# A Mamba2 layer between two mixtures of LoRA experts: x projected two steps further ahead and transposed on VectorE and by DMA

## The chip, the cores and the metric

One core of a Trainium2 chip runs the whole program. The metric is the device time of one execution in microseconds, the median of three runs. Everything is float32; the large products are made of three passes over rounded high parts and remainders (float32r).

## The reference

```python
x = x + 0.5 * ffn(layernorm(x))        # base_W, 8 LoRA experts of rank 16, top 2
x = x + attn(layernorm(x))
x = x + 0.5 * ffn(layernorm(x))
# attn, for x of [4, 256, 512]:
proj = x @ in_proj_w.T                  # gate 8192, xBC 8192+2*8*128, dt 128
xBC = silu(depthwise_conv4(xBC)); x, B, C = split(xBC)
dA = softplus(dt + dt_bias) * A; cs = cumsum(dA)        # chunks of 128 tokens
Y = (C.B * exp(cs_l - cs_s) * tril) @ (x * dt) + carried state + x * D
out = rms_norm(Y * silu(gate), per group of 1024) * norm_w @ out_proj_w.T
```

There are 128 heads of 64 channels in 8 groups; a group shares its B and C.

## The kernel before

Three phases run one after the other: a feed-forward block, the mixer, and a feed-forward block. The mixer takes some 1,430 of the 1,625 us and goes through 8 groups. A group has 16 steps (`STEPS`): a step is one channel tile of 128 channels (two heads, j = st//2) and one half of the tokens (512 tokens, two batches, hf = st%2). Every engine has its own order of work, written out by hand in `steps` and `tail`, and the engines meet at semaphores only.

The projections into the convolution are counted in units, 20 for a group (`UNITS`): 4 for B and C, and then one for each step's x. In a step st, unit st+5 is projected (`ip.project`, L842), taken out of PSUM by ScalarE (`ip.evacuate`, L865), given its three other taps by VectorE (`tap`, L882), passed through a tanh on ScalarE (`tanh_conv`, L1094) and made into silu on VectorE (`silu_conv`, L1240). The result stays in `acc`, which has 4 places.

TensorE's order in a step is: `transpose_x` (L1441: four transposes of 128x128 of x into the bank T_BANK), `ip.project` (12 matmuls), `project_gate` (L1451, 12 matmuls), `project_out` (L1482, 12 matmuls, from step 8 of the first group on) and `mix_tokens` (L1461, 16 matmuls; it raises the semaphore y). Between two groups, in `tail`, it projects units 1 to 5 of the next group, makes the products of B and C (`b_dot_c`, L1426) and sums squares over channels (`sum_over_channels`, L1501).

VectorE's order in a step is: `skip_y` (L1274) of the step before, which waits for y; `make_mix` (L1254); `scale_x` (L1264), x times dt out of T_BANK; the three taps; `silu_gate` (L1283); `silu_conv`; in odd steps `split_wo` (L1288); and in the steps 1 to 8 `add_quads` (L1305) and `add_group` (L1312). GpSimd's order in a step is: `mask_diagonals` (L1016), whose first half (L1021) waits for the rows of cs and its second half (L1025) for y; `gate_y` (L1030) of the step before; `remainder_w` (L837); `split_tile` (L1035); `sum_squares` (L1041). ScalarE: `decay_from_first` (L1100), `round_w` (L831), `evacuate`, `square` (L1133), `round_tile` (L1127), `decay_from_second` (L1111), `tanh_gate` (L1122), `tanh_conv`. SyncE issues all DMAs in one order: in a step the weights of the projection (`load_w`, L816), the rows of cs two steps ahead (`load_cs`, L973), and in odd steps `load_wo`.

Semaphores start at one, so 1 + STEPS * g + n reads "n steps of group g are done". `step_slot_freed` waits for the step before last, as most tiles have two places.

Of the kernel before, what the change touches and what calls it, by code (L numbers as in the profile page):

```python
# [605 lines left out]
class DtPart:  # L606
# [22 lines left out]
    def sync(self, sp):  # L629
# [161 lines left out]
class InProj:  # L791
# [3 lines left out]
    def __init__(self, nc, ctx, m, w_in, conv_w, conv_b, d_skip):  # L795
        def sb(name, shape, dt=F32):
# [4 lines left out]
            "const_in", "nw_in", "const", "proj", "gate", "xt", "y", "cb", "out", "ss",  # L801
# [14 lines left out]
    def load_w(self, sp, g, w):  # L816
        if not (first(g) and w < 3):
            sp.wait_ge(self.s["wlo"], 1 + WPG * g + w - 2)
        sp.dma_start(self.w_raw[:, w % 3, :, :], self.w_in[g, w, :, :, :]).then_inc(self.raw_in[w % 3], 16)
# [11 lines left out]
    def round_w(self, act, g, w):  # L831
        act.wait_ge(self.raw_in[w % 3], 16 * (WPG // 3 * g + w // 3 + 1))
        w_freed(act, self.s, g, w)
        self.nc.scalar.activation(self.w_hi[:, w % 3, :, :], self.w_raw[:, w % 3, :, :],  # L834
                                  ACT.Copy).then_inc(self.s["whi"], 1)
# [19 lines left out]
    def conv_constants(self, dve, g):  # L855
# [7 lines left out]
        dve.wait_ge(s["const"], 1 + 5 * g + 2)  # L863

    def evacuate(self, act, g, u):  # L865
# [34 lines left out]
def mixer_phase(nc, m, ip, norm_w, w_out, ncs_dram, next_ln):  # L900

    with ExitStack() as ctx:
# [4 lines left out]
        wo_in = [ctx.enter_context(nc.semaphore(f"mx_wo_in{i}")) for i in range(2)]  # L907
        cs_in = [ctx.enter_context(nc.semaphore(f"mx_cs_in{i}")) for i in range(2)]
# [17 lines left out]
        sq = sb("sq", [P, 2, HALF])  # L926
# [3 lines left out]
        B_UNIT, C_UNIT = 0, 1  # L930
# [677 lines left out]
```

## Time and profile before

| | |
|---|---|
| median of 3 runs | 1625.21 us (1624.32 to 1627.58) |
| profiled execution, its own time | 1627.01 us |
| span of the profiled execution | 1625.2 us, mean granted TensorE clock 0.989 |
| busy share of the span | TensorE 96%, VectorE 76%, GpSimd 65%, ScalarE 62% |
| transposes of x on TensorE (L1447) | 512, 84.3 us busy |
| DMA | 131.65 MB, 16 queues 24.3% busy |

The span runs from the first to the last instruction; the execution's own time is 1.8 us longer. Busy time of an engine is the union of its instructions; matmuls overlap each other, so that the sum of their durations is more than TensorE's busy time, and the distance from one start to the next is what a matmul costs. An instruction's duration holds what it waits inside, for a port for example, but not its wait for a semaphore, which the profile shows as idle time before it.

### The profile page before, as it was taken

To read this page: it belongs to the slowest core of one execution; us is meant where nothing else is said; L and a number is where in the kernel's file an instruction comes from. 1 tells how busy PE (TensorE), PEld (TensorE's weight loads), DVE (VectorE), ACT (ScalarE), POOL (GpSimd) and SP (SyncE) were. 2 spreads that over 40 slices of the span, in tenths; PEclk is the share of its full clock that TensorE was granted. 3 is DMA by queue.
4 is the path that set the end of the run, shared out by engine and by line. 5 is a ranking of instruction groups with operands and counts; after the bars stand their busy time and mean duration, and the time that the engine had idled before them with its cause. 6 is when DMAs were issued, how large, how long until landed. Compare 5 with 4: busy or idle time off the path is not lost. (4 is left out here: it accounts for less than half of the span.)

```text
span 1625.2 us, 25474 instructions
## 1 busy us (share of the span) xinstructions
PE 1564.3 (96%) x8296; PEld 1226.0 (75%) x8296; DVE 1228.0 (76%) x1689; ACT 1002.3 (62%) x2122; POOL 1052.0 (65%) x790
## 2 busy tenths in 40 slices
PE   6979999999999999999999999999999999999979
PEld 4657777777777777777777777777777777777757
DVE  6688877787778877887688877887688877887565
ACT  4357765666666665666666665666666665666431
POOL 2017874788757874788657874787657874787620
PEclk9899999999999999999999999999999999999989
DMA  3033321323222221222212321223222221322011
GB/s 118 1 103 103 107 91 59 92 91 92 78 72 92 92 92 59 91 92 92 78 72 92 92 91 59 92 92 92 78 75 88 92 92 59 98 86 84 20 40 53
DMA packets 73658, 131.65 MB, mean 81 GB/s; under 512 B 10944, under 2 KB 10944, under 8 KB 73280
## 3 DMA queue, kind: packets, MB, share of 16 engines
q1 hardware_dynamic: 73536, 130.09, 24.3%
q8 instruction: 68, 1.11, 0.3%
q14 instruction: 54, 0.44, 0.1%
HBM read 127.44 MB, written 2.62 MB: 80 GB/s over the span
## 5 line engine op out<-in xcount | busy, mean ns | idle before, releaser
L892 DVE SCALAR_TENSOR_TENSOR mx_acc<-bank,mx_cw,mx_acc 128x510 f32<-128x510 f32 (+2 forms) x480 | 358.3, 746 | 160.8 <-ACT mx_acc L877 149.5
L159 PE MATMUL bank<-h_hi,mx_w_hi 128*128 128x512 f32 x1152 | 465.6, 404 | 4.4 <-DVE mx_acc L892 2.3
L161 PE MATMUL bank<-h_hi,mx_w_lo 128*128 128x512 f32 x1152 | 453.1, 393 | 0.0
L160 PE MATMUL bank<-h_lo,mx_w_hi 128*128 128x512 f32 x1152 | 450.2, 391 | 0.0
L1108 ACT ACTIVATE mx_mix<-mx_csb,mx_gncs 128x256 f32<-128x256 f32 x512 | 218.9, 499 | 284.3 <-PE bank L1478 281.3
L1033 POOL TENSOR_TENSOR mx_y<-mx_y,mx_sg 128x512 f32<-128x512 f32 x128 | 338.4, 2644 | 59.7 <-DVE mx_y L1280 51.7
L839 POOL TENSOR_TENSOR mx_w_lo<-mx_w_raw,mx_w_hi 128x512 fp32r<-128x512 f32 x144 | 187.4, 1302 | 111.0 <-ACT mx_w_hi L834 111.0
L161 PEld LDWEIGHTS bank<-h_hi,mx_w_lo 128*128 128x128 f32 x1152 | 216.9, 188 | 48.5
L159 PEld LDWEIGHTS bank<-h_hi,mx_w_hi 128*128 128x128 f32 x1152 | 217.3, 189 | 47.8 <-issue 6.5
L160 PEld LDWEIGHTS bank<-h_lo,mx_w_hi 128*128 128x128 f32 x1152 | 217.7, 189 | 41.5
L1262 DVE TENSOR_TENSOR mx_mix<-mx_mix,mx_cbt 128x1536 f32<-128x1536 f32 x128 | 224.5, 1754 | 0.0
L1025 POOL TENSOR_SCALAR_AFFINE_SELECT mx_mix<-mx_csb 128x512 f32<-128x512 f32 x128 | 89.9, 702 | 202.0 <-PE bank L1478 202.0
L877 ACT ACTIVATE mx_acc<-bank,mx_cb,mx_cw 128x512 f32<-128x512 f32 x160 | 124.2, 777 | 140.9 <-PE bank L161 140.9
L159 PE MATMUL bank<-mx_wo_hi,mx_yt_hi 128*128 128x512 f32 x512 | 203.4, 397 | 7.3 <-POOL mx_yt_lo L1038 7.3
L1038 POOL TENSOR_TENSOR mx_yt_lo<-mx_y,mx_yt_hi 128x512 fp32r<-128x512 f32 x128 | 167.3, 1307 | 58.2 <-ACT mx_yt_hi L1131 58.0
L161 PE MATMUL bank<-mx_wo_hi,mx_yt_lo 128*128 128x512 f32 x512 | 202.0, 394 | 0.0
L160 PE MATMUL bank<-mx_wo_lo,mx_yt_hi 128*128 128x512 f32 x512 | 200.5, 392 | 0.0
L1021 POOL TENSOR_SCALAR_AFFINE_SELECT mx_csb<-mx_csb 128x512 f32<-128x512 f32 x128 | 123.2, 963 | 68.1 <-DMA mx_csb<-cs_rows 68.1
L1280 DVE SCALAR_TENSOR_TENSOR mx_y<-mx_acc,mx_dh,bank 128x512 f32<-128x512 f32 x128 | 95.3, 745 | 88.9 <-PE bank L1478 88.8
L1118 ACT ACTIVATE mx_mix<-mx_mix,mx_gncs 128x128 f32<-128x128 f32 x512 | 162.1, 389 | 0.0
L1474 PE MATMUL bank<-mx_mix,mx_xd 128*64 128x256 f32 x1024 | 160.5, 392 | 0.0
L1046 POOL TENSOR_TENSOR mx_ssum<-mx_ssum,mx_sq 128x512 f32<-128x512 f32 x112 | 148.2, 1323 | 1.1 <-ACT mx_sq L1140 1.1
(163 smaller groups left out, 2203.7 us busy)
## 6 DMA issues: line engine op xcount, KB each, us to landing
mx_csb<-cs_rows SPq DMA_DIRECT2D x128, 512.0 KB, 4.0
mx_w_raw<-in_w_in SPq DMA_DIRECT2D x144, 256.0 KB, 4.0
mx_wo_raw<-in_w_out SPq DMA_DIRECT2D x64, 256.0 KB, 4.2
res<-in_x SPq DMA_DIRECT2D x8, 256.0 KB, 5.0
f_base_raw<-in_base_wt SPq DMA_DIRECT2D x2, 1024.0 KB, 6.1
out<-res SPq DMA_DIRECT2D x8, 256.0 KB, 2.0
f_a_raw<-in_lora_a SPq DMA_DIRECT2D x2, 256.0 KB, 3.8
f_lb_raw<-in_lora_b SPq DMA_DIRECT2D x2, 256.0 KB, 6.2
```

Of the source, the lines that this page charges most:

```text
L159: nc.tensor.matmul(out, w_hi, x_hi, start=first, stop=False)
L160: nc.tensor.matmul(out, w_hi, x_lo, start=False, stop=False)
L161: return nc.tensor.matmul(out, w_lo, x_hi, start=False, stop=last)
L839: self.nc.gpsimd.tensor_tensor(self.w_lo[:, w % 3, :, :], self.w_raw[:, w % 3, :, :], self.w_hi[:, w % 3, :, :].bitcast(F32), ALU.subtract ...
L892: self.nc.vector.scalar_tensor_tensor(dst, src[:, :, 0:SEQ - k], self.cw[:, c, TAPS - 1 - k:TAPS - k], dst, ALU.mult, ALU.add).then_inc(s[ ...
L1033: nc.gpsimd.tensor_tensor(y[:, st, :], y[:, st, :], sg[:, st % 2, :], ALU.mult).then_inc(s["yg"], 1)
L1038: nc.gpsimd.tensor_tensor(yt_lo[:, p % 2, :, :], y_tile(q, hf, t), yt_hi[:, p % 2, :, :].bitcast(F32), ALU.subtract).then_inc(s["ylo"], 1)
L1046: nc.gpsimd.tensor_tensor(ssum[:, i, :], ssum[:, i, :], sq[:, i, :], ALU.add).then_inc(s["ssum"], 1)
L1108: nc.scalar.activation(mix[:, i, hd, b, 0:SEQ], csb[:, i, hd, b * SEQ:(b + 1) * SEQ], ACT.Exp, bias=gncs[:, tile, head:head + 1], scale=-1.0)
L1118: last = nc.scalar.activation(mix[:, i, hd, b, SEQ:PAIR], mix[:, i, hd, b, SEQ:PAIR], ACT.Exp, bias=gncs[:, tile, head:head + 1], scale=-1.0)
L1262: nc.vector.tensor_tensor(a, a, both, ALU.mult).then_inc(s["mix"], 1)
L1474: nc.tensor.matmul(Y_BANK[i][rows, c0:c0 + SEQ], xd[:, i, 2 * b, hd, :], mix[:, i, hd, b, 0:SEQ], start=True, stop=False)
```

## The change

Three things are changed together.

1. The lead of the projections goes from 5 to 7 units (`LEAD`, `ahead`): step st projects, evacuates and convolves unit st+7, so that units 0, 1 and 2 of the next group are made in the steps 13 to 15, and units 3 to 6 in the tail. Ahead of the first step of the first group stand units 3 to 6 too. The weights are loaded, rounded and split in a new order (`weight_order`), B's two halves before C's two.
2. TensorE transposes x no longer. VectorE transposes the squares of 32x32 of a unit into `th` (`turn_squares`), SyncE writes that tile to memory (`move_out`) and reads it back in four DMAs, one for each row of squares, into the new tile `xt` (`move_in`). `scale_x` reads `xt` in SBUF, where it read T_BANK.
3. The copies of the products of B and C (`keep_bc`) go from VectorE to ScalarE. The tile `sq` is gone: the squares go into `sg`, and `square` stands after `tanh_conv`. The decays read their constants from `m.ncs`, without the copy `gncs`. The loop of SyncE over the groups is written out.

```diff
+LEAD = 7
+def ahead(g, st):
+    u = st + LEAD
+    return (g, u) if u < UNITS else (g + 1, u - UNITS)
...
+def first_needed(g, st):
+    if st % 2 == 1:
+        return (g, 3 + st + 1) if st < STEPS - 1 else (g + 1, 2)
+    j = st // 2 + 2
+    return (g, 2 + 2 * j) if j < XT else (g + 1, (j - XT))
+def weight_order():
+    order = [(0, 0), (0, 1), (0, 2), (0, 4), (0, 3)]
+    for g in range(NG):
+        order += [first_needed(g, st) for st in range(STEPS)] + [(g + 1, 4), (g + 1, 3)]
+    return [(g, k) for g, k in order if g < NG]
...
+        xt = sb("xt", [P, 2, P // SQ, 2 * HB, SQ])
-        sq = sb("sq", [P, 2, HALF])
...
+            def move_out(g, st):
+                i, u = st % 2, st + 4
+                sp.wait_ge(s["turned"], 1 + STEPS * g + st + 1)
+                if not (first(g) and st < 2):
+                    x_moved(sp, *((g, st - 2) if st >= 2 else (g - 1, st + STEPS - 2)))
+                sp.dma_start(x_dram[i, :, :], th[:, u % 2, :]).then_inc(x_out[i], 16)
+            def move_in(g, st):
+                i = st % 2
+                step_slot_freed(sp, s["xd"], g, st)
+                sp.wait_ge(x_out[i], 16 * (XT * g + st // 2 + 1))
+                for q in range(P // SQ):
+                    src = x_dram[i, :, q * P:(q + 1) * P].rearrange("(i r) e -> r i e", r=SQ)
+                    sp.dma_start(xt[q * SQ:(q + 1) * SQ, i, :, :, :].rearrange("r i t c -> r i (t c)"),
+                                 src).then_inc(x_in[i], 16)
...
             def group(g, more):
                 for st in range(STEPS):
+                    ip.load_w(sp, 5 + WPG * g + st + 1)
                     if st + 2 < STEPS:
                         load_cs(g, st + 2)
...
+                    if 3 <= st + 2 < STEPS:
+                        move_in(g, st + 2)
+                    if st + 3 < STEPS:
+                        move_out(g, st + 3)
                 if more:
                     load_late(g + 1)
+                    ip.load_w(sp, 5 + WPG * g + STEPS + 1)
+                    ip.load_w(sp, 5 + WPG * g + STEPS + 2)
+                    for st in range(3):
+                        move_out(g + 1, st)
+                        move_in(g + 1, st)
```

On ScalarE, in `tanh_conv`:

```diff
+                if u >= 6:
+                    act.wait_ge(x_out[u % 2], 16 * (XT * g + (u - 6) // 2 + 1))
```

In a step of ScalarE:

```diff
                     tanh_gate(g, st)
+                    if gu < NG:
+                        tanh_conv(gu, un)
                     if st >= 1:
                         square(g, st - 1)
```

In the tail of ScalarE:

```diff
+                    evacuate(g + 1, 3)
+                    ip.round_w(act, 5 + WPG * g + STEPS)
                     square(g, STEPS - 1)
                     tanh_conv(g + 1, 3)
+                    keep_bc(g + 1, 0)
                     evacuate(g + 1, 4)
+                    ip.round_w(act, 5 + WPG * g + STEPS + 1)
                     tanh_conv(g + 1, 4)
+                    keep_bc(g + 1, 1)
+                    evacuate(g + 1, 5)
+                    tanh_conv(g + 1, 5)
                     root(g)
+                    evacuate(g + 1, 6)
+                    tanh_conv(g + 1, 6)
...
+            def turn_squares(g, st):
+                u = st + 4
+                dve.wait_ge(s["conv"], 1 + UNITS * g + u + 1)
+                nc.vector.transpose(th[:, u % 2, :].rearrange("p (q t c) -> p t q c", t=2 * HB, c=SQ),
+                                    acc[:, u % 4, :, :].rearrange("p b t -> p (b t)")).then_inc(s["turned"], 1)
             def scale_x(g, st):
-                dve.wait_ge(s["xt"], 1 + STEPS * g + st + 1)
+                x_moved(dve, g, st)
                 dve.wait_ge(s["y"], 1 + STEPS * g + max(st - 1, 0))
                 nc.vector.tensor_tensor(
-                    xd[:, i, :, :, :], T_BANK[:, :].rearrange("p (t h c) -> p t h c", h=2, c=HD),
-                    gdt[:, 4 * hf:4 * hf + 4, 2 * j:2 * j + 2].unsqueeze(3).to_broadcast([P, 4, 2, HD]),
-                    ALU.mult).then_inc(s["xd"], 1)
+                    xd[:, i, :, :, :].rearrange("p t h (i c) -> p (h i) t c", c=SQ), xt[:, i, :, :, :],
+                    gdt[:, hf, 2 * j:2 * j + 2, :, :].rearrange("p h i t -> p (h i) t").unsqueeze(3)
+                    .to_broadcast([P, P // SQ, 2 * HB, SQ]), ALU.mult).then_inc(s["xd"], 1)
```

In a step of VectorE, behind `silu_conv` and `split_wo` and ahead of `add_quads`:

```diff
+                    if gu < NG and un >= 4:
+                        turn_squares(gu, un - 4)
```

In the tail of VectorE:

```diff
                     taps(g + 1, 3)
                     silu_conv(g + 1, 3)
                     taps(g + 1, 4)
                     silu_conv(g + 1, 4)
+                    turn_squares(g + 1, 0)
+                    taps(g + 1, 5)
+                    silu_conv(g + 1, 5)
+                    turn_squares(g + 1, 1)
+                    mean_square(g)
+                    taps(g + 1, 6)
+                    silu_conv(g + 1, 6)
+                    turn_squares(g + 1, 2)
```

In a step of TensorE:

```diff
-                    transpose_x(g, st)
-                    if 0 < st < STEPS - 1:
-                        ip.project(pe, g, st + 5)
+                    if gu < NG:
+                        ip.project(pe, gu, un)
                     project_gate(g, st)
```

In the tail of TensorE:

```diff
                     ip.project(pe, g + 1, 3)
                     b_dot_c(g + 1, 0)
+                    ip.project(pe, g + 1, 4)
+                    sum_over_channels(g, 0)
+                    b_dot_c(g + 1, 1)
+                    ip.project(pe, g + 1, 5)
                     sum_over_channels(g, 1)
+                    ip.project(pe, g + 1, 6)
```

## Rows read from the trace of the kernel before

**Rows 1.** The page, busy time of each engine.

```profile
PE 1564.3 (96%) x8296; PEld 1226.0 (75%) x8296; DVE 1228.0 (76%) x1689; ACT 1002.3 (62%) x2122; POOL 1052.0 (65%) x790
```

**Rows 2.** Timeline of TensorE: start us, us, line, idle before; a step, and a tail's beginning.

```profile
705.36 0.66 PE L1447 MATMUL bank<-ident,mx_acc 128*128 128x128 f32 x4
...
706.09 0.40 PE L160 MATMUL bank<-h_lo,mx_w_hi 128*128 128x512 f32 x1
...
715.64 0.66 PE L1447 MATMUL bank<-ident,mx_acc 128*128 128x128 f32 x4
...
808.22 0.50 PE L159 MATMUL bank<-h_hi,mx_w_hi 128*128 128x512 f32 x1
808.56 0.39 PE L160 MATMUL bank<-h_lo,mx_w_hi 128*128 128x512 f32 x1
```

**Rows 3.** Timeline of TensorE: first transposes of four steps, two of the first group.

```profile
130.09 0.66 PE L1447 MATMUL bank<-ident,mx_acc 128*128 128x128 f32 x4 [0.56 <-DVE mx_acc L1244]
...
138.25 0.66 PE L1447 MATMUL bank<-ident,mx_acc 128*128 128x128 f32 x4 [0.56 <-DVE mx_acc L1244]
...
828.39 0.66 PE L1447 MATMUL bank<-ident,mx_acc 128*128 128x128 f32 x4 [1.71 <-DVE mx_acc L1244]
...
836.14 0.66 PE L1447 MATMUL bank<-ident,mx_acc 128*128 128x128 f32 x4
```

**Rows 4.** Timeline of VectorE and GpSimd in a step; then gate_y by line, min/median/max ns.

```profile
706.62 1.75 DVE L1262 TENSOR_TENSOR mx_mix<-mx_mix,mx_cbt 128x1536 f32<-128x1536 f32 x1
706.79 2.74 POOL L1033 TENSOR_TENSOR mx_y<-mx_y,mx_sg 128x512 f32<-128x512 f32 x1 [0.25 <-DVE mx_y L1280]
...
708.29 0.69 DVE L1269 TENSOR_TENSOR mx_xd<-bank,mx_gdt 128x512 f32<-128x512 f32 x1
...
L1033 POOL TENSOR_TENSOR mx_y<-mx_y,mx_sg x128: 1261/2734/2792, 122.6 to 1535.2; 128x512 f32<-128x512 f32 x128
```

**Rows 5.** Timeline of GpSimd and VectorE later in a step; then split_wo by line.

```profile
701.69 1.30 POOL L1046 TENSOR_TENSOR mx_ssum<-mx_ssum,mx_sq 128x512 f32<-128x512 f32 x1
...
702.65 0.89 DVE L1244 SCALAR_TENSOR_TENSOR mx_acc<-mx_th,mx_acc 128x512 f32<-128x512 f32 x1
...
702.94 1.09 POOL L1021 TENSOR_SCALAR_AFFINE_SELECT mx_csb<-mx_csb 128x512 f32<-128x512 f32 x1
...
703.46 1.11 DVE L1290 SCALAR_TENSOR_TENSOR mx_wo_lo<-mx_wo_raw,mx_nw,mx_wo_hi 128x512 fp32r<-128x512 f32 x1
...
L1290 DVE SCALAR_TENSOR_TENSOR mx_wo_lo<-mx_wo_raw,mx_nw,mx_wo_hi x64: 744/1115/1121, 129.9 to 1532.2; 128x512 fp32r<-128x512 f32 x64
```

**Rows 6.** Timeline of VectorE through one even step.

```profile
664.33 0.75 DVE L1280 SCALAR_TENSOR_TENSOR mx_y<-mx_acc,mx_dh,bank 128x512 f32<-128x512 f32 x1
664.99 1.75 DVE L1262 TENSOR_TENSOR mx_mix<-mx_mix,mx_cbt 128x1536 f32<-128x1536 f32 x1
666.66 0.69 DVE L1269 TENSOR_TENSOR mx_xd<-bank,mx_gdt 128x512 f32<-128x512 f32 x1
...
671.18 0.69 DVE L1286 SCALAR_TENSOR_TENSOR mx_sg<-mx_sg,bank 128x512 f32<-128x512 f32 x1 [0.38 <-ACT mx_sg L1125]
...
672.39 0.69 DVE L1309 TENSOR_TENSOR gacc<-bank,gacc 128x512 f32<-128x512 f32 x1
673.19 0.75 DVE L1316 SCALAR_TENSOR_TENSOR res<-gacc,mx_rms,res 128x512 f32<-128x512 f32 x1
```

**Rows 7.** Timeline of ScalarE and VectorE in a tail: one unit.

```profile
811.28 0.78 ACT L877 ACTIVATE mx_acc<-bank,mx_cb,mx_cw 128x512 f32<-128x512 f32 x1 [3.29 <-PE bank L161]
...
812.16 2.31 DVE L892 SCALAR_TENSOR_TENSOR mx_acc<-bank,mx_cw,mx_acc 128x510 f32<-128x510 f32 x3 [1.54 <-ACT mx_acc L877]
...
815.17 1.12 DVE L1244 SCALAR_TENSOR_TENSOR mx_acc<-mx_th,mx_acc 128x512 f32<-128x512 f32 x1 [0.70 <-ACT mx_th L1097]
```

**Rows 8.** The page, DMA issues: KB each, median us from issue to landing.

```profile
mx_csb<-cs_rows SPq DMA_DIRECT2D x128, 512.0 KB, 4.0
...
out<-res SPq DMA_DIRECT2D x8, 256.0 KB, 2.0
```

More of the change, by code:

```diff
@@ L53 @@
 PAIR = SEQ + CH
+SQ = 32
+CONSTS = 7
 NE, RANK = 8, 16
@@ L800, in __init__ @@
         self.s = semaphores(nc, ctx, "mx", [
-            "const_in", "nw_in", "const", "proj", "gate", "xt", "y", "cb", "out", "ss",
+            "const_in", "nw_in", "const", "proj", "gate", "turned", "y", "cb", "out", "ss",
             "evac", "th", "tg", "decay", "sq", "yhi", "whi", "wohi", "gcopy", "root",
@@ L814, in __init__, with load_w @@
         self.acc = sb("acc", [P, 4, HB, SEQ])
[L816 to L819, printed above, removed]
+    def load_w(self, sp, n):
+        if n >= len(ORDER):
+            return
+        if n >= 3:
+            sp.wait_ge(self.s["wlo"], 1 + n - 2)
+        g, k = ORDER[n]
+        sp.dma_start(self.w_raw[:, n % 3, :, :], self.w_in[g, k, :, :, :]).then_inc(self.raw_in[n % 3], 16)
     def load_constants(self, sp, g):
@@ L907, in mixer_phase @@
         wo_in = [ctx.enter_context(nc.semaphore(f"mx_wo_in{i}")) for i in range(2)]
+        x_out, x_in = ([ctx.enter_context(nc.semaphore(f"mx_x_{n}{i}")) for i in range(2)] for n in ("out", "in"))
         cs_in = [ctx.enter_context(nc.semaphore(f"mx_cs_in{i}")) for i in range(2)]
@@ L1148, in keep_first_quad, with keep_bc @@
                 nc.scalar.activation(m.gacc[:, n, :], O_BANK[p % 2][:, :], ACT.Copy).then_inc(s["gcopy"], 1)
+            def keep_bc(g, hf):
+                act.wait_ge(s["cb"], 1 + 2 * g + hf + 1)
+                act.wait_ge(s["mix"], 1 + STEPS * g)
+                banks = Y_BANK if hf == 0 else O_BANK
+                for b in range(HB):
+                    last = nc.scalar.activation(cbt[:, hf, b, :], banks[b][:, 0:PAIR], ACT.Copy)
+                last.then_inc(s["cbt"], 1)
             def root(g):
@@ L1244, in silu_conv @@
                 nc.vector.scalar_tensor_tensor(a, th[:, u % 2, :], 1.0, a, ALU.add, ALU.mult).then_inc(s["conv"], 1)
-            def keep_bc(g, hf):
-                dve.wait_ge(s["cb"], 1 + 2 * g + hf + 1)
-                dve.wait_ge(s["mix"], 1 + STEPS * g)
-                banks = Y_BANK if hf == 0 else O_BANK
-                for b in range(HB):
-                    last = nc.vector.tensor_copy(cbt[:, hf, b, :], banks[b][:, 0:PAIR])
-                last.then_inc(s["cbt"], 1)
             def make_mix(g, st):
@@ L1336, in _ @@
             silu_conv(0, 1)
-            taps(0, 2)
-            taps(0, 3)
-            silu_conv(0, 2)
-            silu_conv(0, 3)
-            keep_bc(0, 0)
-            taps(0, 4)
-            keep_bc(0, 1)
-            silu_conv(0, 4)
+            for u in (2, 3):
+                taps(0, u)
+                silu_conv(0, u)
+            for u in (4, 5, 6):
+                taps(0, u)
+                silu_conv(0, u)
+                turn_squares(0, u - 4)
             def steps(g, more):
                 for st in range(STEPS):
+                    gu, un = ahead(g, st)
                     if st >= 1:
```

263 lines of the change are left out of this document (117 added, 146 removed).

## The prediction

> **What bounds the kernel now.** I read the page first, for the engines' shares, then TensorE's timeline for every start of the transposes, then VectorE and GpSimd side by side through one step, and last the tails between groups. TensorE is busy 96% of the span, the others 62 to 76% [rows 1]. A middle step takes 10.28 us from transposes to transposes, and nothing on TensorE waits in it [rows 2]: 36 matmuls of 512 columns, 16 of `mix_tokens`, four transposes. TensorE waits at two kinds of place: in the first group, whose steps 1 to 7 take 8.16 us with 0.56 of wait for `silu_conv`, and at each group's first transposes, 1.71 us [rows 3]. So at first sight the transposes are what to remove. But VectorE is not idle: in the steps 1 to 8 it goes from one instruction to the next with little between [rows 6].
>
> **What the removal gives.** From the first transposes to the second projection matmul behind them 0.73 us pass, and 0.34 us from first to second matmul where no transposes stand ahead [rows 2]. A step's transposes cost 0.39 us, and TensorE's own need of a middle step falls to 9.89 us. For 128 steps that is 50 us, and the waits of 0.56 and 1.71 us, 16 us in all, may go too. Below I ask what else can be ready at that pace.
>
> **VectorE's price: the squares.** No row shows a VectorE transpose. The nearest rows are the passes of 512 columns, 0.69 us from PSUM and 0.74 us with both sources in SBUF and nobody beside them [rows 4, 5]. I take 0.65 us from start to start (such instructions start some 0.09 us before the one ahead has ended [rows 6]); as bounds I take half of that and twice that, 0.33 and 1.3.
>
> **VectorE's price: the port.** `gate_y` on GpSimd alone takes 1.26 us, in a step 2.74: it starts at 706.79 beside `make_mix` (706.62 to 708.37, two tiles in SBUF) and ends 1.2 us behind it [rows 4]. It has stood still. `scale_x` at 708.29 lasts 0.69 all the same: it reads a PSUM bank and one tile in SBUF. Later in the step, where VectorE has two SBUF sources again, they take turns: sum of squares to 702.99, `silu_conv` stretched by 0.2 until it is over, mask (1.09), then `split_wo` 1.11 against 0.74 alone, since the mask that waited went first [rows 5]. The new `scale_x` has two sources in SBUF. By that pattern `gate_y`, which has waited since `skip_y`, goes when `make_mix` ends, and `scale_x` waits for it: from 708.29 to `gate_y`'s end at 709.53 it is 1.24, less 0.14 (`silu_conv` had 0.34 to that end and was stretched by 0.2): 1.1 us in each step. Bounds: 0, if VectorE goes on ahead, and 1.26. The Trainium skill states the same ("SBUF — State Buffer", "Who interferes with whom": a VectorE instruction with two SBUF inputs contends with a GpSimd instruction that reads SBUF, and the loser blocks fully); the rows agree. Its "VectorE: DVE Perf Modes", in the table on the errata, gives 62 cycles less for an SBUF source than for PSUM, so `scale_x` would be 0.06 us shorter and the kernel 8 us at most; rows 4 show no such difference (1.75 us for 1536 columns in SBUF and 0.69 for 512 from PSUM lie on one line), and I leave it out.
>
> **VectorE's step, from skip_y's start.** `skip_y` 0.66, `make_mix` to 2.33, `scale_x` blocked to 4.0, taps 2.22, `silu_gate` and `silu_conv` 1.21, some 0.2 until the tanh is there: 7.6. Even step: turn to 8.3, `add_quads` 0.80 to 9.1, `add_group` behind the mask, to 10.0. Odd step: the squares are now made behind the last tanh, so `sum_squares` asks at 7.5, just ahead of `split_wo`, which is blocked to 8.8, ends at 9.4; turn 10.05, add 10.85, `add_group` 11.5 (durations: [rows 5, 6, 7]). Mean 10.75. From below: the port itself. GpSimd's six instructions of a step need it 6.2 us (four of 1.25, from 1.26 and 1.30, and two masks of 0.6, which is 1.09 less what L1021 waited for `silu_conv`), VectorE's two-source ones 3.9 (1.67, 0.62, 0.60, half of 0.66, 0.67): 10.1. I take 10.6. In the steps 1 to 8 VectorE is then the bound and not TensorE with 9.89. In the steps 9 to 15 the adds are gone (8.3 even, 10.05 odd): TensorE's 9.89 holds. `keep_bc` on ScalarE stands in the tail alone.
>
> **The boundary.** Count from the start of the first projection behind step 15 (808.22 in rows 2). Five projections, the B.C products and the sums lie on TensorE up to the first `mix_tokens` before and after, and step 1 began at 27.92 (836.14); less 0.41 and 1.71 it could begin at 25.8 [rows 3]. VectorE's chain: from a unit's evacuation to its silu 3.89 us, and 0.6 for that [rows 7]. Unit 3: evacuated at 3.1, done 7.6. Unit 4: evacuated behind `keep_bc` (0.8, estimated from the 0.78 of an evacuation) at 7.6, done 12.1, turned 12.8. Unit 5: TensorE has it at 12.3, done 16.9, turned 17.5. Unit 6 is queued on ScalarE behind `root`, which waits for `mean_square`, which stands behind that turn: evacuated 17.9, done 22.4, turned 23.1. Then `make_mix` 24.8, `scale_x`, blocked by the remainder of a weight, 26.6; mixing takes 1.5: step 1 begins at 28.1. The DMAs of squares 0 lie in parallel: 2.0 us out [rows 8], at most 4.0 back, from 12.8 to 19.5.
>
> What is late next is SyncE. The rows of cs for step 2 were asked for 20 us ahead; now they stand behind `move_out` and `move_in` of squares 2, and `move_in` waits for `scale_x`(0), 26.6. With five issues of 0.48 ahead of it the load goes out at 29.1, lands at 33.2 [rows 8], and is masked at 33.9. `decay_from_first`(2) on ScalarE waits for that, and behind it in that queue the evacuation of unit 8 (36.1) and the tanh of gate 1. VectorE, done with `scale_x`(1) at 33.7, waits for its taps until 37, and comes to `scale_x`(2) at 48.0, where TensorE could mix from 46.4. Step 3 begins at 49.6; VectorE has no slack and sets the pace through `scale_x`(8): 48.0 + 6 x 10.6 = 111.6, step 9 at 113.2, and with 7 x 9.89 and 0.3 behind the odd step 9 the group ends at 182.7, against 27.92 + 15 x 10.28 = 182.2. Plus 0.5, seven times: plus 3.5. With 10.1 and 11.0 for the step it is minus 17 and plus 21 over seven groups.
>
> **The first and the last group.** Ahead of the first step VectorE's chain holds two more units of 3.89 and 0.6 us and three turns of 0.65, 11 us, less some 1 us for the copies that leave it: the second step, which began 8.2 us before the 130.09 of rows 3, begins 10 us later. The late cs rows cost 4 more. Its steps 2 to 7 have no adds: 8.25 and 10.05 by the walk, 8.7 to 9.1 a step against 8.16, plus 4. The steps 8 to 15 gain 8 x 0.39, minus 3; waits that overlap, minus 2: plus 13 (8 to 16). In the last group two projections less (12 matmuls, 2.74 us each) are left for the steps 13 and 14: minus 5.5. The other phases don't change.
>
> Sum: 13 + 3.5 - 5.5 = plus 11. The profiled execution takes 1627.0 us for its span of 1625.2, 1.8 above the median of the runs; so 1638, and 1636 by the median; I say 1637.
>
> **Rivals.**
> - A, the port doesn't bite: `scale_x` stays at 0.62 because VectorE keeps its turn. Then VectorE's step is 9.3 (8.9, and 9.7 where `split_wo` isn't held up either), TensorE's 9.89 holds in all steps, and a group takes 27.0 + 15 x 9.89 and 1.3 for the late cs rows, 176.7: minus 5.5 x 7 = 38; first group plus 8, last minus 5.5: 1590. For it: `make_mix` itself is never held up in rows 4. Against it: the turns in rows 5. It decides from 0.5 us of blocking down. 20%.
> - B, the cs rows come in time, or their wait is covered: each boundary and the first group gain 3.8: 8 x 3.8 = 30, 1607. For it: a landing of 4.0 us is a median, and ScalarE has 3 us to spare in a middle step. Against it: the order of SyncE's queue is fixed, and the step's data are needed 5 us before the load can land. 15%.
> - C, the squares take 1.3: VectorE's every turn is 0.65 longer: 3 in seven tails, 6 in the VectorE-bound steps of seven groups, 10 in the first group, (21 + 42 + 10) x 0.65 = 47: 1684. For it: no row shows the instruction. Against it: all other passes of 512 columns take 0.69 to 0.75 [rows 4 to 6]. 10%.
> - D, the forecast: VectorE and the port take TensorE's place, 1620 to 1656. 55%.
>
> **How the numbers follow.** A measurement of this kernel can tell some 0.2%, 3 us. A and most of B lie on the faster side, with the lower end of D (its bound of 10.1): 0.20 + 0.13 + 0.04 = 0.37 faster. Within 0.2% lie the rest of B and a little of D, 0.09; slower 0.54. The range reaches from A to the upper end of D, 1590 to 1662; D's own is 1620 to 1656.
>
> **What would show it.** In the changed kernel's profile: `scale_x` at 1.7 us rather than 0.69 shows the port, the squares at 0.7 the turn. TensorE's steps should be 9.9 us in the second half of a group and 10.6 in the first; its waits at `mix_tokens`, for xd; in step 1 of each group GpSimd's first mask waits for the DMA of cs, and ScalarE behind it. The first group should end some 13 us later than before, the busy share of TensorE fall to about 93%. I am wrong if `scale_x` stays short, if the steps 1 to 8 hold 9.9, or if the squares take more than 1 us. The sign rests on the step of 10.6 against 9.89.

## The result

The changed kernel takes 1671.35 us (median of four runs, 1666.7 to 1674.0) against 1624.99 us for the kernel before beside it: a ratio of 1.0282, interval 1.0265 to 1.0298. It is slower by 46 us. I had predicted plus 11, and the measured time lies 9 us above my range.

The page of the changed kernel, busy time of each engine; it answers to [rows 1]:

```profile
span 1672.2 us, 24276 instructions
## 1 busy us (share of the span) xinstructions
PE 1535.6 (92%) x7784; PEld 1188.9 (71%) x7784; DVE 1453.3 (87%) x1801; ACT 1014.2 (61%) x2154; POOL 1073.0 (64%) x790
```

TensorE works less and waits more; VectorE has gone from 76% to 87%. VectorE by line, after (busy us, mean ns | idle ahead of it):

```profile
L1329 DVE TENSOR_TENSOR mx_mix<-mx_mix,mx_cbt 128x1536 f32<-128x1536 f32 x128 | 234.4, 1832 | 0.0
L1343 DVE TENSOR_TENSOR mx_xd<-mx_xt,mx_gdt 128x512 f32<-128x512 f32 x128 | 207.6, 1622 | 0.0
L1364 DVE SCALAR_TENSOR_TENSOR mx_wo_lo<-mx_wo_raw,mx_nw,mx_wo_hi 128x512 fp32r<-128x512 f32 x64 | 106.1, 1658 | 0.0
L1335 DVE STREAM_TRANSPOSE mx_th<-mx_acc 128x512 f32<-128x512 f32 x128 | 90.5, 707 | 2.7
```

`scale_x` (L1343) takes 1.62 us where [rows 4] had 0.69, and `split_wo` (L1364) 1.66 where the one of [rows 5] had 1.11. The squares (L1335), with a single input, take 0.71. Who holds `scale_x` up is seen when the two engines are laid side by side in a step; first VectorE, then GpSimd, both after:

```profile
1081.14 1.75 DVE L1329 TENSOR_TENSOR mx_mix<-mx_mix,mx_cbt 128x1536 f32<-128x1536 f32 x1
1082.81 1.79 DVE L1343 TENSOR_TENSOR mx_xd<-mx_xt,mx_gdt 128x512 f32<-128x512 f32 x1
```

```profile
1081.31 2.74 POOL L1089 TENSOR_TENSOR mx_y<-mx_y,mx_sg 128x512 f32<-128x512 f32 x1 [3.48 <-DVE mx_y L1354]
1084.01 1.72 POOL L870 TENSOR_TENSOR mx_w_lo<-mx_w_raw,mx_w_hi 128x512 fp32r<-128x512 f32 x1
```

`gate_y` waits for `make_mix` (to 1082.89), then `scale_x` for `gate_y` (to 1084.05), then the remainder for `scale_x` (to 1084.60): here they take turns. In the steps 9 to 15 `scale_x` is shorter in places, 1.11 us, so that 1.62 is a mean.

**Where the 46 us lie.** From TensorE's timeline I took the start of each step's first `mix_tokens` matmul; an interval is that of a step less that of the step ahead. Sums over the profiled executions:

| stretch | before | after | difference |
| --- | --- | --- | --- |
| start to step 15 of group 0 | 260.2 | 273.3 | +13.1 |
| step 0 of groups 1 to 7 (the boundary) | 27.7 each | 28.70, then 32.75 to 33.77 | +33.2 |
| steps 1 to 8 of these groups | 82.5 each | 85.0 to 85.6 | +20.4 |
| steps 9 to 15 of groups 1 to 6 | 72.0 each | 69.3 each | -16.4 |
| steps 9 to 15 of group 7 | 69.3 | 62.5 | -6.8 |
| behind the last `mix_tokens` | 92.4 | 95.9 | +3.5 |

Sum +47.0, the difference of the two spans. The last row need not be of the change: the kernel of experiment 5 has the same code there and 92.4 us in its profile. The boundary is the largest row. VectorE in the one from group 4 to 5, where TensorE's first projection of it (L162) starts at 1020.78:

```profile
1021.72 1.80 DVE L1364 SCALAR_TENSOR_TENSOR mx_wo_lo<-mx_wo_raw,mx_nw,mx_wo_hi 128x512 fp32r<-128x512 f32 x1
1023.44 0.74 DVE L1354 SCALAR_TENSOR_TENSOR mx_y<-mx_acc,mx_dh,bank 128x512 f32<-128x512 f32 x1
1024.29 1.27 DVE L1397 TENSOR_SCALAR mx_dh<-mx_d_raw 128x8 f32<-128x8 f32 x1
1025.47 2.84 DVE L1400 TENSOR_SCALAR mx_gdt<-dtt 128x64 f32<-128x64 f32 x4
1028.35 2.31 DVE L924 SCALAR_TENSOR_TENSOR mx_acc<-bank,mx_cw,mx_acc 128x510 f32<-128x510 f32 x3
1031.35 0.69 DVE L1319 SCALAR_TENSOR_TENSOR mx_acc<-mx_th,mx_acc 128x512 f32<-128x512 f32 x1 [0.69 <-ACT mx_th L1155]
```

`skip_y`(15) starts 2.7 us behind TensorE's projection, behind a blocked `split_wo`; then `dh` takes 1.27 and the four small gdt copies 2.84 us, and only then come unit 3's taps. Of the four copies two take 0.20 us, and the two that fall beside an instruction of GpSimd 1.33 and 1.35. GpSimd at that time, and the copies by line (min/median/max ns):

```profile
1024.26 1.27 POOL L1089 TENSOR_TENSOR mx_y<-mx_y,mx_sg 128x512 f32<-128x512 f32 x1 [1.29 <-DVE mx_y L1354]
1025.65 1.32 POOL L870 TENSOR_TENSOR mx_w_lo<-mx_w_raw,mx_w_hi 128x512 fp32r<-128x512 f32 x1
1026.93 1.31 POOL L1094 TENSOR_TENSOR mx_yt_lo<-mx_y,mx_yt_hi 128x512 fp32r<-128x512 f32 x1
...
L1400 DVE TENSOR_SCALAR mx_gdt<-dtt x32: 201/208/1348, 99.0 to 1403.0; 128x64 f32<-128x64 f32 x32
```

`dh` is not new: in the kernel before it takes 1.29 us at the same place, but there `skip_y`(15) starts 0.12 us behind the projection, the one gdt copy takes 0.22, and unit 3 is done 8.1 us behind the projection.

Why is `skip_y`(15) late? It isn't simply the lag of the steps 1 to 8, where `skip_y` starts 4.1 to 5.7 us behind the end of its mixing. In step 14 this is down to 0.3 to 0.6 us in the groups 1 to 6, and in step 15 it is 2.5 to 2.9: most of it arises in that one step. By its rows GpSimd's mask stands beside `make_mix` and takes 2.17 us, the evacuation on ScalarE behind the mask comes late, VectorE idles 2.91 us for it, and `split_wo` is blocked besides. In step 15 of group 0 the mask, ahead of `make_mix`, takes 0.64 us (from 265.53), the evacuation comes 2.4 us earlier against the mixing, and `skip_y` is in time. First VectorE, then GpSimd, at the end of group 4:

```profile
1011.95 2.21 DVE L1329 TENSOR_TENSOR mx_mix<-mx_mix,mx_cbt 128x1536 f32<-128x1536 f32 x1
...
1018.11 2.31 DVE L924 SCALAR_TENSOR_TENSOR mx_acc<-bank,mx_cw,mx_acc 128x510 f32<-128x510 f32 x3 [2.91 <-ACT mx_acc L909]
...
1012.49 2.17 POOL L1077 TENSOR_SCALAR_AFFINE_SELECT mx_csb<-mx_csb 128x512 f32<-128x512 f32 x1
```

TensorE in the boundary:

```profile
1028.48 0.95 PE L1565 MATMUL bank<-ones,mx_ssum 128*128 128x1 f32 x8
1032.10 1.22 PE L1506 MATMUL bank<-mx_acc 128*128 128x256 f32 x2 [2.68 <-DVE mx_acc L1319]
...
1035.68 0.63 PE L164 MATMUL bank<-h_hi,mx_w_lo 128*128 128x512 f32 x1
...
1038.59 0.39 PE L164 MATMUL bank<-h_hi,mx_w_lo 128*128 128x512 f32 x1
```

It waits 2.68 us for unit 3's `silu_conv`, and comes back slow: the same matmul takes 0.63 us, and 0.39 from 1037.7 on. The windows show the clock with it (busy us of PE, PEld, DVE, ACT, POOL with instructions, then the granted clock, 0.50 being 1.2 and 1.00 being 2.4 GHz, DMA share and GB/s):

```profile
1026.00:1029.00 3.00, 3.00 (x18) 2.53 (x16) 2.96 (x3) 0.20 (x1) 3.00 (x3) 1.00 0.51 189
1029.00:1032.00 3.00, 0.42 (x4) 0.34 (x4) 2.23 (x4) 1.31 (x4) 0.47 (x1) 0.78 0.00 0
1032.00:1035.00 3.00, 2.90 (x9) 2.54 (x10) 2.19 (x4) 1.27 (x3) 1.66 (x2) 0.50 0.00 0
1035.00:1038.00 3.00, 3.00 (x10) 2.33 (x9) 1.50 (x3) 1.39 (x3) 0.79 (x2) 0.59 0.00 0
```

And in step 1 the rows of cs are late, as foretold; GpSimd's mask of step 2:

```profile
1059.85 1.01 POOL L1077 TENSOR_SCALAR_AFFINE_SELECT mx_csb<-mx_csb 128x512 f32<-128x512 f32 x1 [5.66 <-DMA mx_csb<-cs_rows]
```

### The profile page after: what moved, and what is told of

Same layout as the page of the kernel before. It is cut to its first block and busy times, and to the rows that moved or that the text cites. A ratio compares the mean times of both kernels' runs of the same rounds, so it can differ in the third digit from the quotient of the medians.

```text
span 1672.2 us, 24276 instructions
## 1 busy us (share of the span) xinstructions
PE 1535.6 (92%) x7784; PEld 1188.9 (71%) x7784; DVE 1453.3 (87%) x1801; ACT 1014.2 (61%) x2154; POOL 1073.0 (64%) x790
## 5 line engine op out<-in xcount | busy, mean ns | idle before, releaser
L162 PE MATMUL bank<-h_hi,mx_w_hi 128*128 128x512 f32 x1152 | 472.5, 410 | 4.8 <-DVE mx_acc L924 2.0
L1089 POOL TENSOR_TENSOR mx_y<-mx_y,mx_sg 128x512 f32<-128x512 f32 x128 | 305.4, 2386 | 117.7 <-DVE mx_y L1354 117.6
L1166 ACT ACTIVATE mx_mix<-mx_csb,ncs 128x256 f32<-128x256 f32 x512 | 218.7, 498 | 225.1 <-POOL mx_csb L1077 225.1
L870 POOL TENSOR_TENSOR mx_w_lo<-mx_w_raw,mx_w_hi 128x512 fp32r<-128x512 f32 x144 | 231.6, 1609 | 145.5 <-ACT mx_w_hi L863 144.4
L162 PEld LDWEIGHTS bank<-h_hi,mx_w_hi 128*128 128x128 f32 x1152 | 220.4, 191 | 70.2 <-issue 28.4
L1155 ACT ACTIVATE mx_th<-mx_acc 128x512 f32<-128x512 f32 x160 | 101.0, 632 | 247.7 <-DVE mx_acc L924 247.7
L1329 DVE TENSOR_TENSOR mx_mix<-mx_mix,mx_cbt 128x1536 f32<-128x1536 f32 x128 | 234.4, 1832 | 0.0
L1102 POOL TENSOR_TENSOR mx_ssum<-mx_ssum,mx_sg 128x512 f32<-128x512 f32 x112 | 144.5, 1290 | 126.2 <-ACT mx_sg L1201 126.2
L162 PE MATMUL bank<-mx_wo_hi,mx_yt_hi 128*128 128x512 f32 x512 | 204.0, 398 | 7.3 <-POOL mx_yt_lo L1094 7.3
L1343 DVE TENSOR_TENSOR mx_xd<-mx_xt,mx_gdt 128x512 f32<-128x512 f32 x128 | 207.6, 1622 | 0.0
L1077 POOL TENSOR_SCALAR_AFFINE_SELECT mx_csb<-mx_csb 128x512 f32<-128x512 f32 x128 | 114.5, 895 | 114.0 <-DMA mx_csb<-cs_rows 113.9
L1176 ACT ACTIVATE mx_mix<-mx_mix,ncs 128x128 f32<-128x128 f32 x512 | 162.4, 391 | 0.0
L909 ACT ACTIVATE mx_acc<-bank,mx_cb,mx_cw 128x512 f32<-128x512 f32 x160 | 122.9, 769 | 44.9 <-DVE mx_y L1354 27.6
```

The lines of the kernel that those rows point to most:

```text
L162: nc.tensor.matmul(out, w_hi, x_hi, start=first, stop=False)
L870: self.nc.gpsimd.tensor_tensor(self.w_lo[:, n % 3, :, :], self.w_raw[:, n % 3, :, :], self.w_hi[:, n % 3, :, :].bitcast(F32), ALU.subtract ...
L1089: nc.gpsimd.tensor_tensor(y[:, st, :], y[:, st, :], sg[:, st % 2, :], ALU.mult).then_inc(s["yg"], 1)
L1166: nc.scalar.activation(mix[:, i, hd, b, 0:SEQ], csb[:, i, hd, b * SEQ:(b + 1) * SEQ], ACT.Exp, bias=m.ncs[:, tile, head:head + 1], scale=-1.0)
L1176: last = nc.scalar.activation(mix[:, i, hd, b, SEQ:PAIR], mix[:, i, hd, b, SEQ:PAIR], ACT.Exp, bias=m.ncs[:, tile, head:head + 1], scale=-1.0)
L1329: nc.vector.tensor_tensor(a, a, both, ALU.mult).then_inc(s["mix"], 1)
```

## The experiments

Ten kernels, each a short edit of the changed kernel; the edits are shown in part. The theory: `scale_x`'s turns with GpSimd and the squares fill VectorE's queue, and it comes late to each boundary, where its own small instructions make TensorE wait. The rivals: the squares and their moves alone; the lead and its order alone; the late cs rows.

**1. scale_x's factors in PSUM.** The table gdt lies in a bank of PSUM; it is also what the small copies write.

```
-        gdt = sb("gdt", [P, 2, GH, 2, 2 * HB])
+        gdt = S_BANK[:, P:P + 8 * HB * GH].rearrange("p (f h i t) -> p f h i t", f=2, h=GH, i=2)
...
+                    pe.wait_ge(s["const"], 1 + CONSTS * (g + 1) + CONSTS)
                     sum_over_channels(g, 0)
```

> The scale factors gdt lie in a bank of PSUM, so that scale_x reads one of its two inputs from there; all else is the changed kernel (1671.35 us). Theory (the turns that VectorE and GpSimd take at SBUF make scale_x 1.62 us in place of 0.69, and VectorE's queue sets steps 1 to 8 and the boundary): scale_x falls to 0.7 to 0.9 us, VectorE's pair of steps from 9.95 + 11.39 to at most 9.9 + 10.5, steps 1 to 8 lose 3 to 4 us in each of eight groups, and the boundary of 33.0 us 1 to 3 us more, as VectorE comes to step 15 in time: 1620 to 1645 us. Rival (the squares and their way through memory set the pace, scale_x only waits in their shadow): scale_x is shorter, but steps 1 to 8 and the boundary stay within 1 us of theirs, 1660 to 1672 us. If another operation of VectorE takes the wait over (make_mix or taps behind the same GpSimd instructions), scale_x is short and they are longer by the same amount, also 1660 to 1672 us.

Measured: 1587.64 us, 0.9767 (0.9743 to 0.9792) of the kernel before: 84 us less than the changed kernel, and faster than the one before. VectorE by line:

```profile
L1343 DVE TENSOR_TENSOR mx_xd<-mx_xt,bank 128x512 f32<-128x512 f32 x128 | 86.8, 678 | 0.0
L1400 DVE TENSOR_SCALAR bank<-dtt 128x64 f32<-128x64 f32 x32 | 6.3, 262 | 0.0
```

In steps 1 to 8 TensorE keeps 9.87 us in nearly all; the boundary is 27.6 us in all seven, and `skip_y`(15) starts 0.12 us behind the projection. It gave more than I expected, 84 us for 26 to 51: six boundaries lost 5.1 to 6.1 us each and not 1 to 3, and the steps 1 to 8 lost 5.9 us a group and not 3 to 4. Both rivals fall. The 84 us hold the copies too: each takes 0.26 us here, and none is held up.

**2. The lead alone**, x transposed by TensorE as before, with one gdt copy and no moves.

```
+                    transpose_x(g, st)
...
-                    turn_squares(g + 1, 0)
```

> The projections two steps ahead, the weight order and the B.C copies on ScalarE as in the changed kernel; x is transposed by TensorE at the head of each step and scaled out of PSUM, as in the kernel before, with one gdt copy and no moves through memory. Theory (squares, port and moves are the loss, the lead is not): TensorE sets every step at 10.28 us again, scale_x is 0.69 us, the interval of step 0 is 27.7 to 30 us, the first group is 8 to 13 us later, the last one 4 to 6 us earlier: 1625 to 1645 us. Rival (the lead and the order of work that it brings at a group's boundary are the loss): the interval of step 0 stays at 32 to 33 us and the time, with TensorE's 0.39 us a step back, is 1665 us or more.

Measured: 1632.55 us, 1.0039 (1.0021 to 1.0057). All steps from the second group on are 10.28 us and the boundaries 28.1. The lead with the B.C copies on ScalarE is not what lost the 46 us; by itself it gives nothing and costs some 8: the first mixing comes at 127.1 us for 119.9, each boundary is 0.4 longer, and the last group is shorter.

**3. No transposition of x**: squares and moves left out, `scale_x` reads constants.

```
             def turn_squares(g, st):
+                pass
...
             def move_out(g, st):
+                pass
```

> The changed kernel without the transposition of x: VectorE's 128 squares of 0.71 us and both DMAs of each are left out, and scale_x reads a buffer of constants in SBUF, in the same layout. Theory (port and squares each take their part of VectorE's step; the moves hold up the cs rows of step 2): VectorE's pair of steps falls by 1.4 us, to 9.9 + 10.1, steps 1 to 8 lose 3 to 4 us and the boundary with step 2's late rows 3 to 5 us in each group: 1605 to 1635 us, while scale_x stays at 1.5 us or more. Rival (the port alone is the loss, the squares are hidden in VectorE's idle time): within 10 us of the changed kernel, 1660 to 1672 us. Rival (lead and boundary order alone): the interval of step 0 stays above 32 us, 1645 to 1665 us.

Measured: 1630.67 us, 1.0034 (1.0022 to 1.0046), inside the theory's range, but not by its parts. The steps are 9.87 us, so that the steps 1 to 8 lost 6.3 us a group and not 3 to 4; `scale_x` is 1.68. The boundary stays at 32.8 us in six groups and is 34.2 in the first, which I had expected only if the lead and its order were the loss, and experiment 2 excludes that: without squares VectorE still comes to it behind a blocked `split_wo`, `skip_y`(15) starting 3.6 to 3.8 us behind the projection, and two of each four gdt copies take 1.3 us. So it comes late though TensorE sets the pace of the loop. TensorE's waits from 805 to 850 us:

```profile
PE bank L1489 <- DVE mx_acc L1305: 2.7, 1, 2.7
PE bank L1489 <- DVE mx_y L1336: 1.4, 1, 1.4
PE bank L1517 <- DVE mx_xd L1325: 1.3, 1, 1.3
```

So the boundary's loss doesn't need the squares.

**4. The cs rows of step 2 ahead of the moves.**

```
                 if more:
+                    load_cs(g + 1, 2)
                     load_late(g + 1)
```

> The changed kernel with the cs rows of a group's step 2 issued at the head of the group's boundary, ahead of the moves of x, instead of behind them. Theory (VectorE's idle 3.5 us ahead of its taps in step 1 comes from these rows): the mask of step 2 no longer waits 5.7 us, TensorE's wait at steps 1 and 2 of each later group falls by 2 to 3 us: 1650 to 1660 us. Rival (VectorE is behind anyway and the rows are only the last of several waits): 1664 to 1672 us. By my forecast's own rival the gain would be 4.3 us a group, 1641 us.

Measured: 1658.01 us, 1.0207 (1.0182 to 1.0231): 13 us less, 1.9 a group. The rows' lateness is real, but TensorE still waits 2.3 us for `scale_x`(0), and step 1 takes 11.5 us in groups 1, 2, 4 and 6 without a wait in it. There its clock is low; the windows in group 4:

```profile
856.00:859.00 3.00, 1.24 (x10) 1.01 (x12) 2.96 (x4) 1.87 (x6) 3.00 (x3) 0.87 0.04 12
859.00:862.00 3.00, 3.00 (x13) 2.05 (x10) 2.83 (x5) 2.04 (x5) 1.08 (x2) 0.56 0.60 162
```

In groups 3, 5 and 7 a step of 11.3 us with a wait of 1.3 for `scale_x` comes at step 4 instead, and the later intervals of 11.4, at steps 6 and 8, remain.

**5. The gdt copies behind the first turn.**

```
                     turn_squares(g + 1, 0)
+                    token_constants(g + 1)
```

> The changed kernel with the four gdt copies of the next group, which head_constants issues behind skip_y(15) and ahead of taps(3), moved behind the first turn_squares of the boundary, where VectorE waits for unit 5's first copy anyway. Theory (the 2.8 us of these copies stand between skip_y(15) and unit 3; TensorE waits 2.7 us for unit 3's silu_conv at b_dot_c and its clock falls for it): that wait is gone, the granted clock stays high in the boundary, and the interval of step 0 falls from 33.0 to 28 to 30 us in each of six groups; steps 1 to 8 stay as they are: 1640 to 1655 us. Rival (skip_y(15) is late by VectorE's lag in any case, and TensorE waits there instead): the interval stays above 32 us, 1665 us or more.

Measured: 1648.72 us, 1.0148 (1.0131 to 1.0165), 23 us less. The interval of step 0 is 28.8 to 29.6 us in all seven, and at their new place all four copies take 0.17 to 0.21 us. TensorE waits 0.6 us for `silu_conv` where it had waited 2.7, and the windows from group 3 to 4 hold the clock:

```profile
830.00:833.00 3.00, 3.00 (x17) 2.51 (x16) 2.62 (x4) 1.39 (x3) 2.88 (x3) 1.00 0.80 257
833.00:836.00 3.00, 2.39 (x17) 2.14 (x16) 2.57 (x3) 2.31 (x5) 1.99 (x3) 1.00 0.00 0
836.00:839.00 3.00, 3.00 (x16) 2.50 (x15) 2.23 (x4) 1.39 (x3) 1.83 (x3) 1.00 0.02 5
```

This alone takes 3.8 of the 5.4 us off a boundary, though `skip_y`(15) is as late as ever (828.37, in a boundary whose mixing of step 15 began at 824.3). The steps 1 to 8 don't change as a sum (85.0 to 85.7 us a group).

**6. PSUM, copies and cs rows early.** gdt in PSUM; its copies at the end of step 15.

```
+                    if st == STEPS - 1 and more:
+                        token_constants(g + 1)
...
+                    load_cs(g + 1, 2)
```

> gdt in PSUM (1587.64 us by itself), and besides its copies put at the end of step 15 ahead of skip_y(15), and the cs rows of step 2 at the head of the boundary. Theory: TensorE's wait of 0.9 us at b_dot_c in each boundary goes, and so does the one interval of 11.3 us in group 5: 1578 to 1586 us. Rival (VectorE is not what TensorE waits for there, or the copies cost the same one place earlier): 1586 to 1590 us.

Measured: 1584.88 us, 0.9758 (0.9742 to 0.9775). The interval of 11.3 us is gone, but the boundaries stay at 27.63: neither of TensorE's two waits there has changed. In the boundary from group 3 to 4:

```profile
PE bank L1543 <- DVE mx_xd L1345: 1.2, 1, 1.2
PE bank L1515 <- DVE mx_acc L1321: 0.9, 1, 0.9
```

The wait of 0.9 us at `b_dot_c`, which the theory had go, stays, and unit 3 is done 8.8 us behind the projection in both kernels: copies of 0.26 us each, with `skip_y`(15) in time, hold up nothing. By the two intervals this kernel can't be told from that of experiment 1.

**7. PSUM and no squares**: the edits of 1 and 3 together, so x is not transposed.

> gdt in PSUM and x not transposed: the squares and their moves through memory are left out, scale_x reads a buffer of constants. With the three kernels that are measured this is the fourth of a square (port or no port, squares or none). Theory (VectorE's queue is the bound only when both costs are in it): the steps are TensorE's 9.87 us with and without squares, only the first group, where VectorE sets the steps, is shorter, by 5 to 10 us, and each boundary by up to 1 us: 1572 to 1583 us; so the squares cost 5 to 15 us here and 40.7 us where scale_x is held up. Rival (the two costs simply add): 1547 us.

Measured: 1575.08 us, 0.9692 (0.9676 to 0.9708). The square is full:

| | squares | none |
| --- | --- | --- |
| gdt in SBUF | 1671.35 | 1630.67 |
| gdt in PSUM | 1587.64 | 1575.08 |

The squares cost 41 us beside the port and 13 without it; the port costs 84 us beside the squares and 56 without. They don't add. In the steps TensorE hides what VectorE has below 19.75 us for two: with either cost alone they are 9.87 us. The port without squares costs its 56 us elsewhere, 44 in the seven boundaries and 9 in the first group.

**8. PSUM and two turns** in place of one.

```
+                nc.vector.transpose(th[:, u % 2, :].rearrange("p (q t c) -> p t q c", t=2 * HB, c=SQ),
+                                    acc[:, u % 4, :, :].rearrange("p b t -> p (b t)")).then_inc(s["turned"], 1)
+                dve.wait_ge(s["turned"], 1 + 2 * (STEPS * g + st) + 1)
```

> gdt in PSUM and every squares instruction issued twice (0.71 us more for VectorE in each of 128 steps). Theory: with one turn VectorE's queue needs 19.0 us for a pair of steps 1 to 8 against TensorE's 19.75, so 0.7 of the 1.4 us added to a pair show there, 22 us in eight groups, some 5 us more in the first group and up to 1 us at each boundary: 1608 to 1622 us. Rival (VectorE has slack throughout once the port is free): 1588 to 1595 us. Rival (every VectorE microsecond counts): 1587.6 + 90 = 1678 us.

Measured: 1633.23 us, 1.0043 (1.0026 to 1.0060): 46 us for 90 us of work, and 11 us above the range. The pairs of steps went to 10.33 + 10.19, as expected (0.77 us a pair), though the steps 1 to 8 as a whole lost 3.9 us a group for 2.8; I had sized the boundaries too low, 29.1 us, 1.5 more, where TensorE's wait for `scale_x`(0) grew from 1.2 to 2.7, and the first group, 8 us more.

**9. gate_y on 8 columns**, gdt in SBUF; y is left ungated in the other columns.

```
-                nc.gpsimd.tensor_tensor(y[:, st, :], y[:, st, :], sg[:, st % 2, :], ALU.mult)
+                nc.gpsimd.tensor_tensor(y[:, st, 0:8], y[:, st, 0:8], sg[:, st % 2, 0:8], ALU.mult)
```

> The changed kernel with GpSimd's gate_y on 8 of its 512 columns; the other columns of y are left ungated, and all else, gdt in SBUF too, is as in the changed kernel. It asks whether GpSimd is what holds up scale_x. Theory (both inputs of scale_x lie in SBUF, and it waits for gate_y to end there): scale_x falls from 1.62 to 0.7 to 0.9 us, VectorE's pair of steps to below TensorE's 19.75 us: 1580 to 1600 us, near the kernel with gdt in PSUM. Rival (scale_x with both inputs in SBUF and this order of squares is slow by itself): it stays at 1.5 us or more, 1660 us or more; rival (GpSimd's other instructions, the remainder of the weights above all, move forward and take gate_y's place): 1.1 to 1.5 us, 1620 to 1650 us.

Measured: 1596.26 us, 0.9820 (0.9804 to 0.9835). VectorE and GpSimd by line:

```profile
L1343 DVE TENSOR_TENSOR mx_xd<-mx_xt,mx_gdt 128x512 f32<-128x512 f32 x128 | 101.9, 796 | 0.0
```

```profile
L870 POOL TENSOR_TENSOR mx_w_lo<-mx_w_raw,mx_w_hi 128x512 fp32r<-128x512 f32 x144 | 236.5, 1643 | 152.8 <-ACT mx_w_hi L863 152.7
L1089 POOL TENSOR_TENSOR mx_y<-mx_y,mx_sg 128x8 f32<-128x8 f32 x128 | 179.4, 1402 | 122.7 <-DVE mx_y L1354 120.9
```

With both inputs in SBUF `scale_x` is fast once GpSimd's instruction is short. So it is GpSimd's turn that it waits out, and not a slow layout. `gate_y` itself still takes 1.40 us for 8 columns: it waits out `make_mix`. The edit also relieves GpSimd's own queue, and `dh` and all the gdt copies take 0.20 us, so not all of its 75 us need be `scale_x`; the first experiment leaves GpSimd's work alone, but shortens the copies too.

**10. The third turn behind scale_x(0)**, on top of experiment 6.

```
                     scale_x(g, st)
+                    if st == 0:
+                        turn_squares(g, 2)
...
-                    turn_squares(g + 1, 2)
```

> As the kernel with gdt in PSUM, its copies at the end of step 15 and the cs rows early (1584.88 us), and the third turn_squares of a boundary placed behind scale_x(0) in place of ahead of make_mix(0). Theory: TensorE's wait of 1.18 us for scale_x(0) falls by the 0.63 us from one start to the next of this instruction, 4 to 5 us over eight groups, and x of step 2 is still there in time: 1578 to 1582 us. Rival (step 0's VectorE work, longer by the same time, gives it back at step 1 or 2): 1584 to 1586 us.

Measured: 1581.86 us, 0.9735 (0.9721 to 0.9748), the lowest median of a full kernel here. The boundary is 26.9 us, 0.7 less than in experiment 6, and the wait there 0.44 for 1.18. But the profile gives these 5 us back: in the first group the interval of step 2 is 12.95 us for 8.33 and step 15 comes 3.8 us later than in experiment 6, and the stretch behind the last mixing is 2.2 longer, so that its span is 1.2 us longer. With intervals of time that overlap by 0.0006, a gain of the whole kernel over experiment 6 isn't shown, only that of the boundary.

## Why the prediction was wrong

The sign, and the mechanism of the steps, were right; the boundary's term was not. By its steps:

- **Transposes off TensorE**: a step's own need was given as 9.89; the steps 9 to 15 take 9.87. Right.
- **The squares**, 0.65 taken, 0.71 measured (start to start 0.64): right; rival C is out. The Trainium skill's page "SBUF — State Buffer", section "Who interferes with whom", says that a VectorE instruction with at most one SBUF input doesn't contend, outside the modes that use two ports; the squares (0.707 mean) and `scale_x` from PSUM (0.678) agree. `dh` and the gdt copies in SBUF, with one tensor input, do wait; in which mode they ran no run here shows.
- **The port at scale_x**: 1.24 less 0.14 foretold; mean 1.62 against 0.69, 0.94 more. Right, and experiments 1 and 9 show the cause: both inputs in SBUF, and a GpSimd instruction beside them.
- **VectorE's step** by the walk, 10.0 even and 11.5 odd: measured 9.94 and 11.39. I took 10.6, between the walk's mean of 10.75 and the lower bound; measured are 10.67, and the difference is 0.4 us a group. For steps 1 to 8 together I had 85.0 (21.4 to mixing 2, and 6 x 10.6), measured 85.0 to 85.6.
- **The cs rows late**: right in place (the mask's wait of 5.66 us, TensorE's behind it); taking it away gave 1.9 us a group where rival B had 3.8: VectorE's intervals of 11.39 come back at steps 6 and 8, and in four groups step 1 loses 1.6 us at the lower clock.
- **First group** +13: measured +13.1, of it 9.5 ahead of the first mixing where 10 had been foretold. **Last group** -5.5: the table's -6.8 for the steps 9 to 15 of group 7 holds 2.7 of the transposes' gain, so it is -4.1 there. The 3.5 us behind the last mixing were not foreseen, and are not shown to come from the change.
- **The boundary: wrong.** The step that failed is "Unit 3: evacuated at 3.1, done 7.6". My walk counted VectorE's chain from the evacuation, 3.89 + 0.6, and left out what stands ahead of it in VectorE's queue: `skip_y`(15), 2.6 to 3.0 us behind the projection in the groups that are late, then `dh` 1.27 and four gdt copies of 2.84. I had not priced the change from one gdt copy to four at all, nor that they too can be held up by GpSimd. Unit 3 was done 11.2 to 11.5 us after the projection's start in the groups 2 to 7, not 7.6. TensorE then waited 2.7 us at `b_dot_c`, its clock fell to 0.50, and its matmuls took 0.63 for some 5 us. The interval of step 0 became 32.8 to 33.8 where my walk gives 28.1 (26.6, and 1.5 for mixing 15): 5 us in six groups, 30 of the 34 us that I was short.
- **What each part of it costs.** Ahead of group 1 `skip_y`(15) starts 0.22 us behind the projection, all four copies take 0.21, unit 3 is done at 8.8 (still not 7.6), and the boundary is 28.7. With `skip_y`(15) late and the copies out of the way (experiment 5) it is done at 9.2 to 9.5 and the boundary is 29.2 to 29.6; so the copies, held up by GpSimd, are the larger part and the late `skip_y` the smaller. Experiment 1 has neither, and 27.6. In experiment 3 both are there without squares, and the boundary is 32.8. Why the order of mask and `make_mix` differs between the first boundary and the others, and why `skip_y`(15) is late in the first one too in experiment 3, was not traced.
- **Rival A** (the port doesn't bite) was priced at 1590; the kernel in which it doesn't bite takes 1587.64. That is not luck as to the group, 176.7 by the walk and 175.9 measured; but unit 3 is late there too, done at 8.8 us for the 7.6 of the walk.

That the clock falls because of the 2.7 us wait is borne out by experiment 5, as far as it goes: the wait is 0.6, the clock 1.00, the interval shorter. The rows of the boundary into group 3 part the gain. Unit 3 is done at 11.2 us in the changed kernel and at 9.2 in experiment 5, unit 4 at 15.7 and 12.8, unit 5 at 21.8 and 18.2: 2.0 us are unit 3, and 1.6 more come on behind it, where TensorE projects at the lower clock. That these 1.6 are the clock's alone is likely and not shown.

## What to carry to other kernels

When data are moved out of PSUM, count the SBUF inputs of every VectorE instruction that reads them: the second one puts the instruction into GpSimd's turn, and a small table moved to PSUM can take it out again (here 84 us for 1 KB a partition, with the small copies that fill the table). Where a loop ends, list each instruction in the queue of every engine that the next part waits for, small ones too: VectorE came late to the boundary even in experiment 3, where TensorE set the pace of the steps. In the steps either cost alone, port or squares, was hidden below TensorE's 9.87 us, and the two together were not (9.94 and 11.39).

## What was unexpected of the hardware

- A 128x64 copy with a factor takes 0.20 us from SBUF to SBUF, and 1.31 to 1.35 beside an instruction of GpSimd; its mean of 0.628 is neither. Into PSUM it takes 0.26 in every case (255 to 269 ns). `dh`, 128x8, takes 1.27 us in the boundary, as long as the GpSimd instruction beside it (`gate_y`, 1.27 us from 1024.26), and 0.20 in experiment 9, where that one is short. These too wait for GpSimd, with one tensor input.
- GpSimd's instruction that has waited goes ahead of VectorE's next one, which is already queued: `make_mix`, `gate_y`, `scale_x`, remainder, each after the other, in the step shown above.
- TensorE's wait of 2.3 us for `scale_x`(0) was followed by a granted clock of 0.56 and a step of 11.46 us without a wait in group 4 of experiment 4, but not in each group: in the groups 3 and 5 the same wait (2.23 and 2.24) has a step of 9.87 behind it.
